# A mixture-of-experts layer: router and experts merged into one pass over batches of tiles, with the norm on GpSimd

## The reference

```python
def _ln_t(v, eps=1e-5):
    m = jnp.mean(v, axis=-1, keepdims=True)
    s = jnp.var(v, axis=-1, keepdims=True)
    return (v - m) / jnp.sqrt(s + eps)
...
        gathered = jnp.take_along_axis(expert_out, top_i[..., None], axis=2)
        return jnp.einsum('bnk,bnkc->bnc', top_p, gathered)
...
    t = t + _L1_ffn_ref(_ln_t(t), L1_ffn_router_w, L1_ffn_router_b, L1_ffn_expert_w, L1_ffn_expert_b)
```

## Time and profile before

| what | value |
|---|---|
| median of 3 runs | 2795.91 us (2795.01 to 2797.33) |
| the profiled execution | 2797.76 us, its span 2795.8 us |
| router's stage | 2394.6 to 2543.8 us of the span |
| experts' stage | 2543.8 us to the end |
| mean granted clock of TensorE | 0.87 |

### The profile page before, as it was taken

One profiled execution on the slowest core, in us unless ns is written; L12 is line 12 of the kernel. 1 busy time (PEld: TensorE's weight loads), 2 busy tenths in 40 slices (PEclk: granted clock), 3 DMA queues, 4 the chain that ended last, 5 costly groups with the idle time before them and its releaser, 6 DMA issues. The chain is left out here.

```text
span 2795.8 us, 34597 instructions
## 1 busy us (share of the span) xinstructions
PE 2291.9 (82%) x10800; PEld 1298.5 (46%) x10800; DVE 2198.8 (79%) x3516; ACT 1640.6 (59%) x2225; POOL 578.9 (21%) x468
## 2 busy tenths in 40 slices
PE   0684646759760699999999999999999999768887
PEld 0681213747630344444444444444444444654554
DVE  5327889756598778888888888888888888668998
ACT  0113012632227478888888888888888888213665
POOL 0002340002106401210122012210200000004888
PEclk9996866555565799999999999999999999559999
DMA  4600212000004000000000000000000000000111
GB/s 148 222 19 1 120 44 78 0 9 1 1 1 121 5 1 1 1 1 1 1 1 1 1 1 1 1 1 1 1 1 1 1 1 1 9 0 16 34 34 38
DMA packets 81398, 63.93 MB, mean 23 GB/s; under 512 B 11745, under 2 KB 79329, under 8 KB 79729
## 3 DMA queue, kind: packets, MB, share of 16 engines
q1 hardware_dynamic: 74000, 60.28, 6.7%
q10 hardware_dynamic: 7264, 1.94, 0.3%
HBM read 36.97 MB, written 25.17 MB: 22 GB/s over the span
## 5 line engine op out<-in xcount | busy, mean ns | idle before, releaser
L1753 ACT ACTIVATE inner<-banks,key_bias,scales 128x1024 f32<-128x1024 f32 x512 | 617.3, 1206 | 211.0 <-PE banks L1626 205.8
L1875 DVE TENSOR_TENSOR weights_low<-weights,weights_high 128x1024 f16<-128x1024 f32 x512 | 675.5, 1319 | 17.1
L1760 ACT ACTIVATE weights<-inner 128x1024 f32<-128x1024 f32 x512 | 541.1, 1057 | 16.1 <-DVE weights_low L1875 0.3
L1871 DVE CAST weights_high<-weights 128x1024 f16<-128x1024 f32 x512 | 371.1, 725 | 180.7 <-ACT weights L1760 168.1
L1626 PE MATMUL banks<-queries_high,keys_high 128*128 128x512 f16 x1024 | 304.6, 379 | 0.7 <-ACT inner L1753 0.7
L1641 PE MATMUL banks<-weights_high,tokens_low 128*128 128x512 f16 x1024 | 304.6, 379 | 0.0
L1626 PE MATMUL banks<-queries_low,keys_high 128*128 128x512 f16 x1024 | 304.6, 379 | 0.0
L1641 PE MATMUL banks<-weights_low,tokens_high 128*128 128x512 f16 x1024 | 304.6, 379 | 0.0
L1626 PE MATMUL banks<-queries_high,keys_low 128*128 128x512 f16 x1024 | 304.6, 379 | 0.0
L1641 PE MATMUL banks<-weights_high,tokens_high 128*128 128x512 f16 x1024 | 304.5, 379 | 0.0
L1949 POOL CAST sums_high<-sums 128x512 f16<-128x512 f32 x32 | 39.4, 1230 | 1089.8 <-ACT sums L1743 1071.8
(11 more groups left out here) (432 smaller groups left out, 3751.3 us busy)
## 6 DMA issues: line engine op xcount, KB each, us to landing
images_a<-in_x SPq DMA_DIRECT2D x4, 2048.0 KB, 16.6
tokens_scratch<-images_a SPq DMA_DIRECT2D x4, 2048.0 KB, 13.1
images_b<-tokens_scratch SPq DMA_DIRECT2D x32, 256.0 KB, 2.8
mixed_scratch<-images_a SPq DMA_DIRECT2D x4, 2048.0 KB, 13.1
spare<-in_x SPq DMA_DIRECT2D x32, 256.0 KB, 2.9
result<-group_result SPq DMA_DIRECT2D x32, 256.0 KB, 2.3
images_b<-mixed_scratch SPq DMA_DIRECT2D x10, 768.0 KB, 5.3
table<-tables ACTq DMA_DIRECT2D x1, 805.5 KB, 14.3
```

The source lines that it names most:

```text
L1753: act.activation(m.inner[:, t % 2, :], m.pair[t % 2], ACT.Exp, scale=m.fs[:, 1:2], bias=m.kb[:, c // QN % 2, k:k + 1]).then_inc(s.inner, 1)
L1760: act.activation(m.wt[:, t % 2, :], m.inner[:, t % 2, :], ACT.Exp).then_inc(s.outer, 1)
L1871: vec.tensor_copy(m.wH[:, t % DEEP, :], m.wt[:, t % 2, :]).then_inc(s.high, 1)
L1875: vec.tensor_tensor(m.wL[:, t % DEEP, :], m.wt[:, t % 2, :], m.wH[:, t % DEEP, :], ALU.subtract)\
```

## The change

`stage_router` and `stage_experts` become one stage, `stage_ffn`. The groups are cut into batches of 4, 8, 8, 8 and 4. While the experts run over the tiles ("slots", n = 0 to 127) of one batch, the groups of the next are prepared between them, at places that `batch_plan` gives:

- Preparing a group: POOL applies the norm (`normed(t)`, L2216; 127 columns, the last is set to 1 once), PE turns it (`turn`), ACT makes the high part straight from PSUM (`high`) and DVE the low part (`low`), PE makes the logits from both parts with 12 products of 8 columns (`logit`). The turned tokens are not stored in f32 any more; high and low parts lie in a ring of 16 groups.
- The places: in a batch of 32 slots the 8 groups of the next are begun at slots 0, 2, 5, 7, 10, 13, 15 and 18, their logits follow two slots later; the algebra of the gates is cut into 7 pieces, one each ahead of the adds of slots 24 to 30. In the first batch, of 16 slots, the 8 groups are begun in slots 0, 0, 1, 1, 2, 3, 3, 4 and the pieces lie in slots 8 to 14. The first 4 groups and their gates are made ahead of slot 0.
- The combination: DVE takes four experts with four chained multiply-adds of 128 columns, beginning from the token (`add`, L2170); ACT scales the other four as before; POOL adds these in two halves (L2231, 256 columns), then the halves (L2237), then DVE's sum (L2245).
- The biases: the weights are reflected with the matrix `m.house` at the start, so that the normalised tokens' last coordinate is free, and biases are added into that row of the weights. The product of gates and biases with its adds (L2029 to L2105) is gone, and so is the barrier between the two stages.
- SP loads the biases with 2 DMAs instead of 17.

```diff
+BATCHES = [4, 8, 8, 8, 4]
+RING = 16
+SETTLE = 11
+        for i in range(BATCHES[k]):
+            prep.setdefault(at + i * (slots - SETTLE) // BATCHES[k], []).append(first[k] + i)
+        for i in range(7):
+            pieces[at + slots - 8 + i] = k
...
+            def turn(t):
+                pe.wait_ge(s.normed, t + 1)
+                reached(pe, s.low, t - 1)
+                for j in range(GRP):
+                    mm = pe.transpose(m.ps[t % 2][:, j * P:j * P + P], m.ln[:, t % 2, j, :], m.ident)
+                mm.then_inc(s.turned, 1)
...
+            for n in range(NI):
+                expert(n)
+                for t in prep.get(n - 2, []):
+                    logit(t)
+                for t in prep.get(n, []):
+                    turn(t)
...
+            for n in range(NI):
+                scaled(n)
+                for t in prep.get(n - 1, []):
+                    high(t)
+                if n in exps:
+                    exps_of(exps[n])
...
+                add(n, 0)
+                add(n - 1, 2)
+                add(n, 1)
+                add(n - 1, 3)
+                for t in prep.get(n - 1, []):
+                    low(t)
...
-            def residual(g, v):
-                pool.wait_ge(s.reduced, (g + 1) * GRP)
-                pool.tensor_tensor(m.y[:, v], m.y[:, v], group(m.b, g), ALU.add).then_inc(s.result, 1)
...
+            def normed(t):
+                reached(pool, s.turned, t - 1)
                 for j in range(GRP):
...
+                    img = t * GRP + j
+                    e = pool.tensor_scalar(m.ln[:, t % 2, j, 0:D - 1], m.b[:, img, 0:D - 1], m.fac[:, 0, img:img + 1],
+                                           m.fac[:, 1, img:img + 1], ALU.subtract, ALU.mult)
+                e.then_inc(s.normed, 1)
...
+            for n in range(NI + 2):
+                for t in prep.get(n, []):
+                    normed(t)
+                if n < NI:
+                    pool.wait_ge(s.scaled, n + 1)
...
+                    pool.tensor_tensor(m.half[:, n % 2], m.pb[:, n % 3, 0:2], m.pb[:, n % 3, 2:4], ALU.add).then_inc(s.halved, 1)
```

More of the change, by code:

```diff
@@ L292, in memory @@
     with ExitStack() as l2:
[L293 to L298, removed]
+        m.w8 = sb(l2, "expert_weights", [P, EXPERTS * D + EXPERTS])[:, :]
+        m.bias = sb(l2, "expert_biases", [P, EXPERTS * D + EXPERTS])[:, :]
@@ L300, in memory @@
+        m.one = sb(l2, "scaled_sum", [P, 2, D])
+        m.u = sb(l2, "residual_and_scaled", [P, 4, D])
         m.y = sb(l2, "group_result", [P, 2, GRP, D])
[L301 to L307, removed]
@@ L1979, in _, with batch_plan, stage_ffn, logits @@
                         .then_inc(row[c % 2], 16)
[L1982 to L1987, removed]
+BATCHES = [4, 8, 8, 8, 4]
+RING = 16
+SETTLE = 11
+def batch_plan():
+    first = [sum(BATCHES[:k]) for k in range(len(BATCHES))]
+    prep, pieces, exps = {}, {}, {}
+    for k in range(1, len(BATCHES)):
+        at, slots = first[k - 1] * GRP, BATCHES[k - 1] * GRP
+        for i in range(BATCHES[k]):
+            prep.setdefault(at + i * (slots - SETTLE) // BATCHES[k], []).append(first[k] + i)
+        for i in range(7):
+            pieces[at + slots - 8 + i] = k
+        exps[at + slots - 6] = k
+    return first, prep, pieces, exps
+def stage_ffn(nc, held, m, ins, out):
+    s = semaphores(nc, held, "ffn", "loaded cleared biased v factor rooted weights ones normed turned high low logits shifted exp gates "
+                   "tile_d tile_a chain scaled halved paired result stored0 stored1")
+    out_img = out.rearrange("b t h w -> h (b t) w")
+    stored = [s.stored0, s.stored1]
+    first, prep, pieces, exps = batch_plan()
+    LAST = NI + 2
+    batch_of = [k for k, n in enumerate(BATCHES) for _ in range(n)]
+    DBANK, ABANK = [2, 3, 7], [4, 5]
+    order = []
+    for n in range(NI + 1):
+        order += [(n, 0), (n - 1, 2), (n, 1), (n - 1, 3)]
+    order = [(n, e) for n, e in order if 0 <= n < NI]
+    place = {key: i for i, key in enumerate(order)}
+    def logits(k):
+        return m.ps[6][:, k % 2 * 256:k % 2 * 256 + BATCHES[k] * GRP * EXPERTS].rearrange("p (t e) -> p t e", e=EXPERTS)
     with nc.Block() as block:
@@ L2039, in _ @@
[L2039 to L2056, removed]
@@ L2108, in stage_experts @@
[L2108 to L2126 removed]
+                sp.dma_start(m.bias[D - 1:D, 0:EXPERTS * D].rearrange("p (e c) -> p e c", e=EXPERTS),
+                             ins['L1_ffn_expert_b'].unsqueeze(0)).then_inc(s.biased, 16)
@@ new lines, in _ @@
+            pe.wait_ge(s.loaded, 32)
+            for i in range(2):
+                pe.matmul(m.pair[1][:, 512 * i:512 * i + 512], m.house, m.w8[:, 512 * i:512 * i + 512], start=True, stop=True)
+            pe.matmul(m.pair[2][:, 0:EXPERTS], m.house, m.w8[:, EXPERTS * D:], start=True, stop=True).then_inc(s.weights, 1)
+            for t in range(BATCHES[0]):
+                turn(t)
+                if t >= 1:
+                    logit(t - 1)
+            logit(BATCHES[0] - 1)
+            for n in range(NI):
[3 more added lines that the diff above has]
+                for t in prep.get(n, []):
+                    turn(t)
```

330 lines of the change are left out of this document (157 added, 173 removed).

## The result

The changed kernel takes 2835.58 us (median of 4 runs, 2830.51 to 2843.33), the one before 2796.62 us (2795.01 to 2797.57): a ratio of 1.0142, interval 1.0115 to 1.0169. It is 39 us slower; the forecast was 16 us slower. The time lies in the range of 2735 to 2842; the loss is 2.4 times the one forecast. The profiled execution took 2831.95 us, its span 2829.9. The changed part begins at 2393.8 us and so takes 436.1 us, against 401.2.

A forecast was written before the change was run, and what follows sets the result against it. VectorE was taken to bound the old experts' window, about 1.9 us a tile. Start 34.4, batches 70, 202 (two), 79 and 25.8, end 6 made 417.2 us against 401.2, hence 2812 us; range 2735 to 2842.

The forecast's parts named there:

- The norm on GpSimd: Preparing a group: the norm takes 0.41 us a tile, 1.64 a group, with bounds of 0.14 and 0.555.
- The sign: Whole kernel: slower than before, by 16 us; chances 0.48 slower, 0.40 faster, 0.12 within what a measurement can tell.
- The coupling: Preparing slots: norm, turn, tile, scaling and sums wait for each other in a loop; GpSimd stands 2 us.
- the forecast's loops: Preparing slots, upper clock: two slots take 6.8 us or three take 8.6; 21 slots of a batch 63.4.
- The slots without preparation: Full batch: four plain slots at 1.61 us, bound by GpSimd, and seven with algebra at 3.05, 21.4, bound by VectorE.
- the factor: GpSimd's sums: all raised by 1.11 over the older rows, giving 1.61 us a slot; 1.45 without.
- The clock: Preparing slots: half at the lower clock, so a full batch takes 101 us instead of 91.2, the fourth 79.
- Start, first batch, fourth, end: Parts of the sum: start 34.4 us, first batch 70, fourth 79, last slots 25.8 with an end of 6.
- My loop: Preparation counted from the norm through turn, tile and scaling to GpSimd's sums; slots behind it at a plain 1.61 us.
- (3): Preparing slots: looser coupling, GpSimd's own work is the bound; 332 us for the changed part, 2727 in all; 20%.
- (2): Preparing slots: the clock holds at the upper level; 392.2 us for the changed part, 2787 in all; 22%.
- (1): Preparing slots: the lower clock holds through all of them; 452 us for the changed part, 2847 in all; 13%.

The follow-up runs named there:

- norm_mult_add: The changed kernel with GpSimd's norm as multiply and add instead of subtract and multiply, at its old place: 2795.56 us, ratio 0.9998 to the kernel before.
- The filler: The changed kernel with six extra products of 512 columns on TensorE ahead of each turn from slot 16 on: 2833.00 us, ratio 1.0127 to the kernel before.
- pool_early: The changed kernel with its long norm on GpSimd issued two slots earlier (one in the first batch): 2762.42 us, ratio 0.9883 to the kernel before.
- mult_add_early: The changed kernel with the multiply-and-add norm on GpSimd, issued two slots earlier: 2766.96 us, ratio 0.9892 to the kernel before.
- run 28: Not a label of a run: the text says that the loop is run 28 times, for the 28 groups prepared; no time belongs to it.
- bench_pool: The changed kernel with a stage added behind the last, in which GpSimd alone runs norm forms and sums at several widths: 2903.75 us in one run.

## Why the prediction was right in sign and wrong in size

- **The norm on GpSimd** is the step that failed. "The same kind of instruction takes 0.555 us at 256 and 0.697 at 384, which gives 0.41" took multiply and add for subtract and multiply. The group that the sum puts at 1.64 us took 3.2: a norm measured 0.833 in the pass, outside the bounds of 0.14 to 0.555, and the multiply-add form 0.463. norm_mult_add prices the difference at 40 us. With it taken off the measured 39, the change costs nothing, where my sum had 16 with a norm of 0.41: the rest of the sum was 16 us too slow on the median, and 18 in the profiled execution, whose part runs from 2391.0 to 2789.9 us (398.9 against 417.2). Two errors of opposite sign thus made the result. The sign came out right by luck: with a norm near the size that I counted, the change is no slower than the kernel before.
- **The coupling** was right. GpSimd stands behind the norm's slot with `scaled` as releaser, 3.4 us in the preparation shown, where I had 2 (in the whole pass it waits so 61 times, 123 us, not all behind norms), and opening it gave 73 us. By the forecast's loops with the right norm (8.4 and 10.2 us) the 21 preparing slots of a full batch take 76.2 us; the trace has 81. About 31 of these 81 us are at the lower clock, which would make 9 or more at 0.3 us each, so the 5 us left are not a clean price of the clock.
- **The slots without preparation** in a full batch, four plain and seven with a piece of the algebra, took 28.0 us, against 6.4 + 21.4 = 27.8. Plain slots took 1.53 us, between my 1.61 and the 1.45 without the factor. GpSimd's sums of 256 and 128 columns took 0.741 and 0.476 us in the pass and 0.724 and 0.455 alone, so the factor of 1.11 was too high. The Trainium skill's page "SBUF — State Buffer", section "Who interferes with whom", says that an instruction of VectorE with one SBUF input leaves GpSimd alone; the trace agrees to within 5%. Where both inputs are in SBUF VectorE paid: the steps of the algebra on 64 columns (L2144 to L2146) took 0.224 to 0.243 us with GpSimd at rest for at least four fifths of them, and 0.270 to 0.769 (six of seven 0.38 or more) with its instructions beside most of their time. The eleven slots together took what the sum has for them.
- **The clock** was taken at the lower level for half of the preparations, 9.8 us a full batch. It was at it for 37 of 109 us. The filler took 4.8 us off one batch by removing 16 of these; at 0.3 us for each of the 37 it would be 11, an estimate. So the size was about right, by a share and a price that both differed. No run here parts the transposes from the waits beside them, so whether they count as work for the clock is not shown.
- **Start, first batch, fourth, end**: 35.0, 65.4, 88.5 and 28.7 us, forecast 34.4, 70, 79 and 31.8. With the short norm the first two were 34.4 and 61.2: the first batch was counted 9 us too slow. With 6 us each for the two full batches (95 against 101) and 3 at the end that is 24; the fourth batch took 84.6 with the short norm, 6 more than forecast, which leaves the 18. (My sum has 18.4 for its seven pieces where 7 x 2.7 is 18.9; the half microsecond decides nothing.) The trace of the changed kernel shows what the fourth batch lacked in my count. A preparation there has five slots, and GpSimd stands twice in it, the second time two slots later:

```profile
2732.65 0.72 POOL L2231 TENSOR_TENSOR scaled_halves<-scaled 128x256 f32<-128x256 f32 x1 [3.31 <-ACT scaled L2108]
...
2733.83 0.27 PE L2054 MATMUL banks<-expert_weights_high,normed_high 128*128 128x8 f32 x1 [0.95 <-DVE normed_low L2130]
...
2739.61 0.73 POOL L2231 TENSOR_TENSOR scaled_halves<-scaled 128x256 f32<-128x256 f32 x1 [3.89 <-ACT scaled L2108]
```

Between them TensorE waits 0.95 us for the low part, makes the 12 products of the logits and then a tile at the lower clock. My loop had the turn in it, and put the slots behind it at a plain 1.61 us.

- **Rivals.** (3) did not come: the preparing slots stayed coupled. Even with the coupling opened its 2727 us were not reached, 2762 with the long norm (pool_early) and 2767 with the short one (mult_add_early), so GpSimd's own work was not the only bound; only with the logits later as well did the time fall to 2729. (2) and (1) did not come; the clock was between, 0.83 in the full batches. A tenth of the preparations at the lower clock costs 6 us by my own terms (452 - 392.2), not 5.

## What to carry to other kernels

When two engines hand work to each other in program order, write the loop through their queues, and issue the step that opens it one or two slots ahead: that gave 73 us here with no work removed. A price read from another instruction holds only for the same pair of operations, not for its name and shape; measure it alone when it stands in a loop that is run 28 times. An order of TensorE's instructions has to be tried in the version that it is meant for, and read by the waits and the granted clock together: the same shift of the logits gained 38 us in one version and lost 16 in the other. And a sign that comes out right says little when the terms behind it are off by more than the result: take them off one by one, as norm_mult_add does here.

## What the runs showed of the hardware

- GpSimd's scalar form depends on the pair of operations: at 128 columns in f32 subtract and multiply 0.800 us, multiply alone 0.605, multiply and add 0.452; at 512 columns 2.076, 1.564 and 0.774. One operation more can be faster (bench_pool; two factors per token, one for multiply alone). In the pass the change of form alone was worth 40 us.
- The time at the lower clock cost about 0.3 us for each microsecond in three pairs of batches with and without a filler, and 0.47 in a fourth: an estimate, since each comes from single executions. Only TensorE's part of the loop is stretched: its products of 512 columns started 0.43 us apart at the lower clock and 0.23 at the upper (at 2534.8 and 2537.2 us of the changed kernel), while ScalarE's four scalings took 1.14 us at either.
- A VectorE step with both inputs in SBUF can take up to three times as long beside GpSimd's instructions: up to 0.769 us against 0.224 to 0.243 at 64 columns.
- More work on TensorE made the kernel faster: four wide products in each wait for the low part, 14 us less. The same idea ahead of the turns gave nothing beyond the runs' spread (2.6 us).
- Four runs of a version spread over 2 to 13 us, those of the kernel before over 3 to 6. The first batch, the same program in four of the profiled executions, took 65.4 to 65.6 us in three of them and 69.6 in the fourth.
